# Adding MoE outputs into two DRAM tables by indirect accumulating DMAs during the experts, with a shorter router chain

## What is computed

```python
scores = sigmoid(x @ router_w.T)                 # T=4096 tokens, E=32 experts
sc = scores + e_bias
group_scores = top_k(sc.reshape(T, 8, 4), 2)[0].sum(-1)
gmask = the 3 best of the 8 groups
topk_idx = top_k(where(gmask, sc, 0), 4)         # 4 experts for each token
topk_w = scores[topk_idx] / sum * 2.5
C = ceil(1.25 * T / E)                           # 160 places per expert, first come, first served
Xp = x[slots_token].reshape(E, C, d)             # pairs past place 160 are dropped
Y = (silu(Xp @ W_gate) * (Xp @ W_up)) @ W_down   # per expert
out = zeros(T, d).at[slots_token].add(Y * slots_w)
out = out + shared_expert(x)
```

## Time and profile before

| | us |
|---|---|
| median of 3 runs | 2558.71 |
| lowest and highest | 2549.15, 2562.81 |
| span of the profiled execution | 2652.0 |
| of it: before the MoE phase's first DMA | 2018.7 |
| router stage, to the last scatter's landing | 2018.7 to 2342.8 |
| expert stage, to POOL's first step of the combine stage | 2342.9 to 2443.3 |
| combine stage | 2443.3 to 2652.0 |

### The profile page before, as it was taken

One profiled execution on the slowest core, in us unless ns is written; L12 is line 12 of the kernel. 1 busy time (PEld: TensorE's weight loads), 2 busy tenths in 40 slices (PEclk: granted clock), 3 DMA queues, 4 the chain that ended last, 5 costly groups with the idle time before them and its releaser, 6 DMA issues. The chain is left out here.

```text
span 2652.0 us, 39910 instructions
## 1 busy us (share of the span) xinstructions
PE 2029.2 (77%) x12272; PEld 1774.7 (67%) x12272; DVE 1674.2 (63%) x4576; ACT 1081.1 (41%) x2760; POOL 824.7 (31%) x778
## 2 busy tenths in 40 slices
PE   7999999999987996799888889899974555457000
PEld 5877877877866884688888778788874444356000
DVE  8867767667754553477777777777763445445443
ACT  5433333333323331376666666666662111146000
POOL 1222322322320000133333333333320433431776
PEclk9999999999998997799999999999997665679555
DMA  3100000000002123000000000000003111146101
GB/s 120 32 25 24 0 24 24 15 9 24 16 9 94 48 64 106 30 6 17 22 13 13 12 13 16 13 21 12 9 9 128 65 37 35 34 133 204 36 25 30
DMA packets 93344, 103.68 MB, mean 39 GB/s; under 512 B 16670, under 2 KB 84710, under 8 KB 92592
## 3 DMA queue, kind: packets, MB, share of 16 engines
q1 hardware_dynamic: 80912, 97.06, 11.5%
q0 software_dynamic: 12288, 5.08, 0.8%
HBM read 86.55 MB, written 44.04 MB: 49 GB/s over the span
## 5 line engine op out<-in xcount | busy, mean ns | idle before, releaser
L224 POOL TENSOR_TENSOR rwkv_gate<-rwkv_key,rwkv_gate 128x512 f32<-128x512 f32 x128 | 206.3, 1612 | 569.1 <-DVE rwkv_key L406 569.1
L1094 POOL TENSOR_TENSOR mla_probs<-mla_probs,mla_row_inv 128x512 f32<-128x512 f32 x192 | 199.7, 1040 | 471.0 <-DVE mla_row_inv L1391 470.8
L1376 DVE CUSTOM_DVE_ANT_0 mla_masked<-mla_score,mla_mask 128x256 f32<-128x256 f32 (+1 forms) x512 | 157.3, 354 | 164.6 <-PE mla_score L1586 115.0
L291 ACT ACTIVATE rwkv_gate<-rwkv_r 128x512 f32<-128x512 f32 x128 | 76.4, 597 | 417.9 <-DVE rwkv_o_low L343 417.9
L1205 ACT ACTIVATE mla_probs<-mla_masked,mla_least 128x256 f32<-128x256 f32 (+1 forms) x512 | 227.4, 447 | 35.1 <-DVE mla_least L1376 31.1
L392 DVE TENSOR_TENSOR rwkv_kv<-rwkv_v,rwkv_key 128x512 f32<-128x512 f32 x128 | 88.0, 688 | 178.6 <-PE rwkv_v L441 110.5
L2023 POOL DMA_INDIRECT slots<-moe_x_rows,moe_slot_now x128 | 124.8, 975 | 198.1 <-DVE moe_slot_at L2270 110.0
L458 PE MATMUL rwkv_out<-rwkv_w_high,rwkv_o_high 128*128 128x256 f32 x512 | 146.3, 286 | 38.1 <-DVE rwkv_o_low L343 38.1
L1221 ACT ACTIVATE mla_p_high<-mla_pt 128x512 fp32r<-128x512 f32 x192 | 114.3, 595 | 136.7 <-PE mla_pt L1595 132.0
L398 DVE TENSOR_TENSOR_SCAN rwkv_state<-rwkv_decay_w,rwkv_kv 128x256 f32<-128x256 f32 x256 | 163.4, 681 | 4.1
L1586 PE MATMUL mla_score<-mla_k_high,mla_q_high 128*128 128x256 f32 (+1 forms) x512 | 157.6, 308 | 1.8 <-DVE mla_cq_low L1309 1.8
(11 more groups left out here) (360 smaller groups left out, 6597.5 us busy)
## 6 DMA issues: line engine op xcount, KB each, us to landing
moe_w_raw<-in_experts SPq DMA_DIRECT2D x32, 384.0 KB, 4.4
rwkv_w_raw<-in_rkvo SPq DMA_DIRECT2D x16, 512.0 KB, 3.4
slots<-moe_zeros SPq DMA_DIRECT2D x40, 128.0 KB, 1.8
moe_e_rows<-slots SPq DMA_DIRECT2D x32, 160.0 KB, 3.9
slots_out<-moe_y_rows SPq DMA_DIRECT2D x32, 160.0 KB, 3.8
mla_w_raw<-in_mla_heads SPq DMA_DIRECT2D x4, 1152.0 KB, 7.7
rwkv_x_in<-in_x_t SPq DMA_DIRECT2D x16, 256.0 KB, 4.0
rwkv_x_res<-in_x SPq DMA_DIRECT2D x8, 512.0 KB, 3.9
```

The lines of the kernel that those rows point to most:

```text
L224: nc.gpsimd.tensor_tensor(gate[:, c % 2, :], key[:, c % 2, :], gate[:, c % 2, :], ALU.mult).then_inc(gated_done, 1)
L1094: nc.gpsimd.tensor_tensor(unit, unit, row_inv[:, v % 3, 0:len(heads)].rearrange("p (h a) -> p h a", a=1) .to_broadcast([P, len(heads), key ...
L1376: last = nc.vector.tensor_tensor_reduce(out=masked[:, v % 2, i * keys:(i + 1) * keys], in0=score_ps[v % 2][:, i * keys:(i + 1) * keys], in ...
```

## The change

The table `slots` gets wider rows of 289 words (1,156 bytes): the token's 256 features, its 32 weighted scores (zero where the expert isn't chosen), and the token's number. So the expert stage has with its rows the weight (column 256+e, loaded once more by a DMA of its own into `e_weight`, one word per row) and the row to add to. ACT scales while copying. POOL then adds the 2 x 80 rows of an expert to two DRAM tables `sums[0]` and `sums[1]` by two accumulating indirect DMAs. A DMA into a table waits for the last expert's DMA into the same table. The rows of expert e+4 reuse the buffer that holds the indices of expert e, so their load waits until e's additions have landed. `slots_out` with its stores, the gathers and the per-token weights go. The combine stage loads two plain tables per pair and adds them with one operation each. Both tables (4,224 rows) and `slots` are first filled from one row tile `empty`, by 4 large DMAs. In the router, several loops over choices or groups become one operation, casts go, `member` is made before the shared expert's steps; 29 linked steps become 23.

```diff
@@ SP, filling and loading @@
-                    for a in range(SLOTROWS // P):
-                        sp.dma_start(slots_dram[a * P:(a + 1) * P, :], zeros[:, :]).then_inc(slots_zeroed, 16)
+                    half = SLOTROWS // CH2 // 2
+            for a in range(2):
+                sp.dma_start(slots_dram[a * half * CH2:(a + 1) * half * CH2, :]
+                             .rearrange("(b p) d -> p b d", p=CH2),
+                             empty[0:CH2, :].rearrange("p (a d) -> p a d", a=1)
+                             .to_broadcast([CH2, half, ROW])).then_inc(slots_zeroed, 16)
+            for a in range(SUMS):
+                sp.dma_start(sums_dram[a].rearrange("(b p) d -> p b d", p=P),
+                             empty[:, 0:D].rearrange("p (a d) -> p a d", a=1)
+                             .to_broadcast([P, SUMROWS // P, D])).then_inc(sums_zeroed, 16)
             def load_slots(e, i, r):
                 if not (isinstance(e, int) and e < RING):
-                    sp.wait_ge(e_turned, e - RING + 1)
+                    wait_first(sp, e_turned, e - RING + 1, passed)
+                    for a in range(2):
+                        wait_first(sp, y_added[r][a], 16 * i, passed)
                 sp.dma_start(e_rows[:, r, :, :], slot_rows(slots_dram, e)).then_inc(slots_in[r], 16)
-            def store_y(e, i, r):
-                sp.wait_ge(y_copied, e + 1)
-                sp.dma_start(slot_rows(y_dram, e), y_rows[:, r, :, :]).then_inc(y_stored[r], 16)
+                sp.dma_start(e_weight[:, r, :, :], slot_rows(slots_dram, e)[:, :, bass.ds(e + D, 1)],
+                             allow_slow_non_contiguous=True).then_inc(slots_in[r], 16)
             def experts(e, i, r):
                 if is_expert(e + RING):
                     load_w(e + RING, i + 1, r)
-                    load_slots(e + RING, i + 1, r)
-                if late(e):
-                    store_y(*ring_of(i, r, -1))
+                if is_expert(e - 1 + RING) and late(e):
+                    before, i1, r1 = ring_of(i, r, -1)
+                    load_slots(before + RING, i1 + 1, r1)
+            def load_sums(n, i, r):
+                if not (isinstance(n, int) and n < RING):
+                    sp.wait_ge(added, 2 * (n - RING) + 2)
+                for a in range(SUMS):
+                    sp.dma_start(y_in[:, r, a, :, :], sums_dram[a][bass.ds(n * 2 * P, 2 * P), :]
+                                 .rearrange("(t p) d -> p t d", p=P)).then_inc(sums_in[r], 16)
@@ POOL @@
-            def gather(n, i, r):
...
-                for k in range(TOPK):
-                    for t in range(2):
-                        at = t * TOPK + k
-                        nc.gpsimd.indirect_dma_start(
-                            y_in[:, r, t, k, :], None, y_dram,
-                            bass.IndirectOffsetOnAxis(gather_now[:, r, at:at + 1], 0),
-                            bounds_check=SLOTROWS - 1, oob_is_err=False).then_inc(gathered[r], 16)
+            def add_rows(e, i, r):
+                pool.wait_ge(y_copied, e + 1)
+                for a in range(2):
+                    if not (isinstance(e, int) and e < SUMS // 2):
+                        _, before, r2 = ring_of(i, r, -(SUMS // 2))
+                        wait_first(pool, y_added[r2][a], 16 * before + 16, passed)
+                    nc.gpsimd.indirect_dma_start(
+                        sums_dram[r * 2 % SUMS + a],
+                        bass.IndirectOffsetOnAxis(e_rows[:, r, a, IDCOL:ROW].bitcast(U32), 0),
+                        y_rows[:, r, a, :], None, bounds_check=SUMROWS - 1, oob_is_err=True,
+                        compute_op=ALU.add).then_inc(y_added[r][a], 16)
@@ ACT, expert_out @@
-                    act.wait_ge(y_stored[r], 16 * i)
-                nc.scalar.activation(y_rows[:, r, :, :], route_ps[0:CH2, :].rearrange("p (a d) -> p a d", a=2),
-                                     ACT.Copy).then_inc(y_copied, 1)
+                    for a in range(2):
+                        act.wait_ge(y_added[r][a], 16 * i)
+                for a in range(2):
+                    last = nc.scalar.activation(y_rows[:, r, a, :], route_ps[0:CH2, a * D:(a + 1) * D], ACT.Copy,
+                                                scale=e_weight[:, r, a, :])
+                last.then_inc(y_copied, 1)
@@ DVE, router: after the second max_index @@
+                link(v.tensor_tensor(chosen[:, :, :, :],
+                                     counts[:, :].rearrange("p (a b e) -> p a b e", a=1, b=1)
+                                     .to_broadcast([P, BT, TOPK, E]),
+                                     best_at[:, :, 0:TOPK].rearrange("p t (k a) -> p t k a", a=1)
+                                     .to_broadcast([P, BT, TOPK, E]), ALU.is_equal))
+                link(v.tensor_tensor(pair_sum[:, :, :, :], chosen[:, :, 0:2, :], chosen[:, :, 2:4, :], ALU.add))
+                link(v.tensor_tensor(member[:, :, :], pair_sum[:, :, 0, :], pair_sum[:, :, 1, :], ALU.add))
+                dve.sem_inc(member_done, 1)
                 if late(blk):
                     add_shared(blk - 1, i + par - 1, 1 - par)
-                link(v.tensor_copy(expert_at[:, :, :], best_at[:, :, :]))
                 shared_hidden(blk)
-                for k in range(TOPK):
-                    last = v.tensor_tensor(chosen[:, k, :, :],
-                                           counts[:, :].rearrange("p (a e) -> p a e", a=1)
-                                           .to_broadcast([P, BT, E]),
-                                           expert_at[:, :, k:k + 1].to_broadcast([P, BT, E]), ALU.is_equal)
-                link(last)
-                link(v.tensor_tensor(pair_sum[:, :, :, :], chosen[:, 0:2, :, :], chosen[:, 2:4, :, :], ALU.add))
-                v.tensor_tensor(member[:, :, :], pair_sum[:, 0, :, :], pair_sum[:, 1, :, :], ALU.add)\
-                    .then_inc(member_done, 1)
-
-                for k in range(TOPK):
-                    last = v.tensor_tensor(picked[:, k, :, :], chosen[:, k, :, :], score[:, :, :], ALU.mult)
-                link(last)
-                link(v.tensor_reduce(weight_k[:, :, :].rearrange("p t k -> p k t"), picked[:, :, :, :],
-                                     axis=AX.X, op=ALU.add))
+                link(v.tensor_tensor(member_score[:, :, :], member[:, :, :], score[:, :, :], ALU.mult))
...
+                v.scalar_tensor_tensor(x_rows[:, par, :, D:IDCOL], member_score[:, :, :], ROUTE_SCALE,
+                                       weight_inv[:, :].rearrange("p (t a) -> p t a", a=1)
+                                       .to_broadcast([P, BT, E]), ALU.mult, ALU.mult)
+                v.tensor_copy(x_rows[:, par, :, IDCOL:ROW].rearrange("p t a -> p (t a)").bitcast(U32), token_f[:, :])
...
-                last.then_inc(places_read, 1)
+                v.tensor_tensor(place_e[:, :, :, :], chosen[:, :, :, :], places, ALU.mult).then_inc(places_read, 1)
...
-                link(v.tensor_scalar(full[:, :, :], full[:, :, :], -ROUTE_SCALE, ROUTE_SCALE, ALU.mult, ALU.add))
...
+                v.scalar_tensor_tensor(slot_now[:, par, :].rearrange("p (t k) -> p t k", k=TOPK), full[:, :, :],
+                                       PAST_END, slot_f[:, :, :], ALU.mult, ALU.add).then_inc(slots_done, 1)
@@ DVE, combine @@
-                for k in range(TOPK):
-                    for t in range(2):
...
-                        last = nc.vector.scalar_tensor_tensor(
-                            row, y_in[:, r, t, k, :], weight[:, bass.ds((2 * n + t) * TOPK + k, 1)], row,
-                            ALU.mult, ALU.add)
...
+                    pair = total[:, bass.ds(2 * n, 2), :]
+                    nc.vector.tensor_tensor(pair, y_in[:, r, a, :, :], pair, ALU.add).then_inc(chain, 1)
```

151 lines of the change are left out of this document (70 added, 81 removed).

## The result

| | us, median (runs) | lowest to highest |
|---|---|---|
| before, same chip | 2558.71 (7) | 2549.15 to 2564.41 |
| changed | 2570.78 (7) | 2563.30 to 2573.08 |

The ratio is 1.0043, 95% interval 1.0023 to 1.0063: 11 us slower (6 to 16; the medians alone differ by 12), less than the 0.5% that counts as a difference here. The profiled run took 2564.16 us with a span of 2562.4; its lines can be set against the timed runs as they stand.

The account below looks back on a forecast made before the run. Before's combine stage was taken as bound by POOL's gather issues, the changed expert stage by a buffer loop. Fills +24, router -12, experts +132.7 and combine -142.3 sum to +2.4: 2561 us, range 2499 to 2620.

Parts of the forecast that it names:

- Fills, +24: Router stage's start: 14.6 MB from 4 DMAs ahead of block 1's rows, nothing hidden, +24 us (+21 to +38).
- Router chain, -12: Router blocks: DVE's shorter chain makes a block 3 us shorter, limited by POOL's scatters; -12 us taken.
- reasoning by ends: Router gain set between -25 (long waits stay) and 0 (timed runs lack the waits, POOL bounds).
- the case that I set beside it: Router: timed runs lack the long waits, a block takes 23 us, POOL's 21.4 bounds; shortening worth 4 in total.
- Expert stage, +132.7: Expert stage: the loop through the rows' buffers takes 7.3 us an expert instead of 2.7, +132.7 us.
- The round of two turns: Expert stage: copies 5.3, additions 6.0 and load 3.3 make a round of 14.6 us for two experts.
- the low clock: Expert stage: PE, with waits, is less busy than 60% and runs at the low clock; rows to `y_copied` 5.3 us.
- Combine stage, -142.3: Combine stage: 16 pairs at 3.6 us on DVE, loads hidden, 66.4 instead of 208.7 us; -142.3.
- the shorter round: Rival, expert stage: additions land like a scatter, PE at full clock, round 11.4, -46 us, about 2515; chance 0.30.
- The additions hold nothing up: Judges a rival, expert stage: held-up hand-overs or late landing, round 17 to 20, +34 to +75 us; chance 0.24.
- The wider scatter: Rival, router: 1,156-byte rows issued as two pieces, each scatter up to 0.3 longer, +38, 2600; chance 0.06.
- unchanged block periods: Sign in the router stage that would show the prediction wrong: block periods unchanged from before.

Follow-up runs that it names:

- the two pairs of runs: Tables cleared in eighths behind each block's rows: against the changed kernel, 1.0014 to 0.9960; with rings of eight on both sides, slots' fills also moved, 0.9723 to 0.9641.
- the ring of numbers: Changed kernel with tokens' numbers and weights in rings of eight, so row loads wait for PE's turn alone: 2570.76 us, ratio 0.9723 to before.

## Why the prediction was right

2561 was forecast and 2570.78 measured; 11 us above before, where +2.4 was forecast. Most of the 9 us between them are the expert stage's (+6.8) and the fills' (+2.7). The forecast gave only 0.22 to a time within 0.5% of no change, and its range of 2499 to 2620 left the sign open. The terms against what the runs showed:

- **Fills, +24.** +26.4 to the first scatter (two kinds of profiles: 62.7 and 63.0 against 36.3); block 1's turn 27.0 later after the first fill. The estimate of 320 GB/s for the stretch was high: 289 at a share of 0.96. That most of it is not hidden is shown by the two pairs of runs, in which 14 to 23 us went with the tables' fills.
- **Router chain, -12.** -13.7 or -19.2 between the stages of profiles with the hold, by which profile of before is taken; -20 there if the balance is made on one chip (3.7 is 26.4 less 2.7 less 20); -14 on the chip without it, by difference: 11.0 less the 26.7 of fills and the stages' -1.5 (139.5 and -141.0). That last one leans on a profile of before from another kind of chip. The reasoning by ends was half right. I took the long waits for the profiler's; the timed runs of two chips have them. That they end with the scatter's end holds for the last wait of a block, which ends 2 to 3 us behind POOL's last issue; others end up to 13 us ahead of it. But the case that I set beside it came about on the chip of the first result: by their length its timed runs had no such waits, POOL's 20.8 us bound the blocks of the changed kernel, and before's stood only 2 us above (22.8, by difference). The 4 us that I gave for that case did not follow even from its own numbers: 7 x (23 - 21.4) is 11; by difference it was 14.
- **Expert stage, +132.7.** +138.0 and +139.5 (start of the stage to start of the next). The round of two turns was 14.6 by the forecast and 14.5 in the trace, and its parts were off both ways:

| part | forecast | trace |
|---|---|---|
| rows to `y_copied` | 5.3 | 5.5 |
| POOL's start | 0.95 | 0.9 |
| two issues | 2.24 | 3.32 |
| landing | 2.8 | 2.0 |
| load to the next turn | 3.3 | 2.7 |

  An addition's issue was mis-sized: taken for a scatter's 0.97, it is 1.40 to 1.62. The landing and the load were each too dear by 0.6 to 0.8. The ground for the low clock was misread: in the stretch of the earlier trace rows PE was busy for 14.8 of 20 us at 0.63, not less than 60%; the stage came out at 143 of 240 us and 0.53. So the total rests on errors that cancel, and only the structure, a loop through the buffers, was right for the reason given, and PE's low clock came true; the ring of numbers showed it by taking 77 us out. The Trainium skill (DMA: Bandwidth & Descriptors, Anatomy of one DMA) counts setup and completion handling into its fixed 2.0 us, so the estimate of 2.2 us by it, which I set against the landing alone, belongs beside issue and landing together. Those took 2.5 us for the plain write of the same rows (0.92 and 1.6) and 3.4 for the addition (1.40 and 2.0): the trace is near it for the plain write and not for the accumulating one. For the 128 rows they took 2.3, the estimate for them is 2.3 too; the 1.35 of landing alone, which I had said agrees with it, does not.
- **Combine stage, -142.3.** -140.7 and -141.0. A pair took 3.44 to 3.5 us on DVE, 3.6 was forecast; the loads stayed hidden.

The rivals: the shorter round did not come (an addition is dearer than a scatter by 0.5 in the issue and 0.4 in the landing, and PE's clock was the low one). The additions hold nothing up: in the expert stage the changed kernel's round is the same on the chips where the scatters do. The wider scatter costs 0.99 us an issue in place of 0.98. Of the signs to look for, unchanged block periods would have spoken against the forecast; they did change, from about 23 (by difference) to 20.8, and with the hold from about 36.5 to 34.1. One sign fell otherwise than written: block 1's turn came at 2076.64 in a phase that began 7.4 us earlier, that is 3 us later than the 2081 named.

## To carry to other kernels

When work moves from a stage bound by issues into a pipelined one, the question is what its buffers now wait for: here the row's number, 4 bytes that the addition reads last, kept a whole row's buffer taken until an addition had landed, and a 140 us gain became nothing; with a deeper ring for the small fields 77 us of it came back. Clears of new tables stand in the same queue as the loads, and here block 1's rows, issued after them, came 27 us later. A long wait in one profile should be set against a second profile from another chip before it is called an artefact.

## What was not expected of the hardware

- The kernel before takes 2559 to 2562 us on some chips and 2648 to 2655 on others. In the changed kernel (2571 and 2657) the difference is a router block of 20.8 or 34.1 us, with ACT and DVE waiting while POOL issues 128-row scatters back to back. What releases them the profile doesn't show, and the cause is open. Accumulating writes, issued two by two with waits between, bring none of it.
- An accumulating indirect write of 80 rows of 1 KB costs POOL 1.40 to 1.62 us of issue where the plain one costs 0.92 to 1.1. It lands about 2.0 us after the end of its issue, at a DMA share of the stage of 0.46 and of 0.64 alike, and the next one into the same table starts 3.0 to 3.1 us after that end, POOL's own start included.
- A DVE step of 0.17 us takes 0.63 when POOL's elementwise addition of 1.26 us is under way, and ends with it (2432.97 and 2432.94).
